# Graph attention layer on one core: turned adjacency blocks evacuated later in ScalarE's order, first loads in another order

## The chip, the cores and the metric

One NeuronCore of a Trainium2 chip. The metric is device time in microseconds (us). Before the change it is 1793.12 us, the median of three runs (1792.2 to 1793.35).

## What is computed

A graph attention layer over N = 8192 nodes with 128 features and H = 4 heads of 32, then a residual and a layer norm:

```
Wh      = x @ W.T                       (8192, 4, 32)
score_l = sum(Wh * a_l), score_r = sum(Wh * a_r)
e       = leaky_relu(score_l[n] + score_r[m], 0.2), where adj[n, m] + eye > 0, else -inf
out     = elu(softmax(e over m) @ Wh)
y       = layernorm(x + out)
```

adj is an 8192 x 8192 matrix of zeros and ones in float32, 256 MB. Because leaky_relu has two slopes, exp(e) is a product of a factor of n and a factor of m on either side of e = 0. The kernel therefore needs for each head only two 0/1 masks per pair of nodes: adjacent with e >= 0 (`bmask`), and adjacent with e < 0 (`cmask`). Each multiplies its own set of weighted values (`vt`, later read back from DRAM into `vring`) on TensorE.

## The kernel before, in words

**Units of work.** The output rows are cut into 4 chunks of 2048 (two halves of 1024). There are 16 passes of 32 steps, 512 steps in all. Passes 0 to 3 take one half of chunk 0 and two heads each ("narrow"); passes 4 to 15 take a whole chunk and one head ("wide"). A step q covers 256 of the columns m. Per step:

- *compare* (L479 ScalarE, L681 VectorE): makes the 0/1 mask of score_l against score_r into `bmask` from `lrow`, the row scores copied to all partitions. A step is four instructions in a narrow pass and two in a wide one; `on_vector` (L78) says how many of them VectorE does. ScalarE runs AH = 3 steps ahead in its own order (L524), and at most BR = 6 steps ahead of TensorE (L485, L486).
- *mask_b* and *mask_c* on VectorE (L703, L718): and with the adjacency bits, into `bmask` and `cmask`. `cmask` has CR = 3 buffers, so mask_c waits for the products of three steps before.
- *step* on TensorE (L391): 32 products with `bmask`, then the turns of adjacency blocks due in this step, then 32 products with `cmask`.

**Adjacency blocks.** The adjacency comes as 128 blocks of 1024 x 512 float32 (2 MB). SyncE loads a block in two parts into `abuf`, which has two buffers (`load_block`, L216; it waits until the block before the last one has been turned). TensorE turns it, transposed and packed four bits to a byte, into `trp`, a single PSUM bank (`turn_block`, L365). ScalarE copies `trp` into the cache `acache` (`evacuate`, L453). `turn_block(n)` waits for the evacuation of n - 1 (L368), because `trp` has no second buffer. `FIRST_TURNS` and `LATER_TURNS` (L54, L56) set the step in which a block is turned: blocks 2 to 15 in pass 0, blocks 16 to 63 with 2 or 3 steps between them (steps 32 to 144), blocks 64 to 127 with 3 or 4 (steps 148 to 393). ScalarE evacuates a block that was turned in step q at position q + 1 of its own order, behind compare(q + 4). After step 393 no block is left, and passes 13 to 15 have no turns.

**The end of a pass.** VectorE takes the sums from PSUM (L731, L735), which waits for TensorE's last products of the pass; then it weighs, adds and normalises in small pieces over the next steps. In passes 4, 8 and 12 the rows of a finished chunk are normalised in steps 13 to 20 (ScalarE, L502).

**The setup.** The values of x come in 16 groups (`load_x`, L212; a ring of six). TensorE transposes a group and projects it, VectorE takes the scores, ScalarE copies Wh. After every fourth group the row scores of a chunk are transposed, copied (`copy_l` of VectorE, L587) and stored to DRAM (`store_l`, L225). `load_lrow(0)` reads those of chunk 0 back. In SyncE's order it stands behind group 13, with a wait for the store (L286). Then VectorE makes the weighted values (`weigh`, L622; `rest`, L637; `lowest`, L644) together with ScalarE (`highest`, `middle`, L468, L475), for which ScalarE first makes `vv` (L511 to L513). SyncE's list of first loads is L278 to L292.

Each engine works strictly in the order written out by hand in its own block; nothing is reordered.

Of the kernel before, what the change touches and what calls it, by code (L numbers as in the profile page):

```python
# [6 lines left out]
def gat_kernel(nc, x, adj, W, a_l, a_r, out):  # L7
# [10 lines left out]
    NC = N // CHUNK  # L18
# [3 lines left out]
    QUADS = NT // BITS  # L22
# [41 lines left out]
    TURNED = [turned_at(q) for q in range(Q)]  # L64
    assert [n for t in TURNED for n in t] == list(range(AHEAD, NB))


    DIAGONALS = [(c, k // 2, 4 * c + k) for c in range(NC) for k in range(4)]

# [8 lines left out]
    def on_vector(q):  # L78

        w, s = WHERE[q]  # L80
        if s % 4 == 3:
            return 0
        if w == 0:
            return 0 if s < 2 else 2 if s % 2 == 0 and s % 8 != 6 else 1
        if w == 1:
            return 0 if s < 6 else (2 if s % 3 == 0 else 1)
        if narrow(w):
            return 0 if s < 5 else 1 if s % 5 == 0 else 2
        return 0 if s < 6 or s in (10, 17, 22, 29) or (w % 4 == 0 and s in (8, 9)) else 1
# [22 lines left out]
    with ctx:  # L112
# [98 lines left out]
        def _(sp):  # L211
# [13 lines left out]
            def store_l(c):  # L225
                sp.wait_ge(l_copied, c + 1)
                sp.dma_start(l_dram[c].rearrange("h j p -> (h j) p"), l_t[0:H * JC, c]).then_inc(l_stored, 16)

            def load_lrow(w):

                if w >= 2:
                    sp.wait_ge(cmp_act, (w - 1) * STEPS)
                    sp.wait_ge(cmp_dve, ON_VECTOR[(w - 1) * STEPS])
                c, half, h = UNITS[w][0]
                if narrow(w):
                    src = l_dram[c:c + 1, h:h + 2, half * SUB:(half + 1) * SUB].rearrange("o u j n -> o u (j n)").to_broadcast([P, 2, HALF])
                    sp.dma_start(lrow[:, w % 2], src).then_inc(lrow_in[w % 2], 16)
                else:
                    src = l_dram[c:c + 1, h].rearrange("o j n -> o (j n)").to_broadcast([P, CHUNK])
                    sp.dma_start(lrow[:, w % 2].rearrange("p u n -> p (u n)"), src).then_inc(lrow_in[w % 2], 16)  # L240
# [25 lines left out]
            def load_xr(c, half):  # L266
                for s in range(2):
                    sp.dma_start(zz[s::2, half * SUB:(half + 1) * SUB], as_bytes(x, c, half, s)).then_inc(xr_in, 16)
# [8 lines left out]
            sp.dma_start(acol[:, 1:2], a_r.rearrange("h (k o) -> (h k) o", o=1)).then_inc(a_in, 16)  # L277
            for g in range(XG):  # L278
                load_x(g)
                if g in (8, 11, 14, 15):  # L280
                    k = (8, 11, 14, 15).index(g)
                    load_block(k // 2, [k % 2])
                if g == 11:
                    store_l(0)
                if g == 13:
                    sp.wait_ge(l_stored, 16)  # L286
                    load_lrow(0)
            load_xr(0, 0)
            for c in range(1, NC):
                store_l(c)  # L290

            loaded, turned = 2, AHEAD  # L292
            for q in range(Q):
                w, s = WHERE[q]
                while loaded < NB and loaded - 1 <= turned:
                    load_block(loaded)
                    loaded += 1
                if w < JUST_MADE and s % EVERY_STEPS == 1:
                    store_v(q // EVERY_STEPS)
                if JUST_MADE * STEPS <= q + VR - 1 < Q:  # L300
                    load_v(q + VR - 1)
                turned += len(TURNED[q])
                if s == 3 and w + 1 < PASSES:
                    if w == 0:
                        sp.wait_ge(l_stored, 16 * NC)
                    load_lrow(w + 1)
                if w == 2 and s == 4:
                    sp.wait_ge(v_lo, JUST_MADE * NG)
                    load_xr(0, 1)
                if w == 2 and s == 22:  # L310
                    store_y(0, 0, ROWS_DONE[1])
                if w % 4 == 0 and w > 0:
                    c = w // 4
                    if s == 24:
                        for half in range(2):
                            if (c - 1, half) != (0, 0):
                                store_y(c - 1, half, ROWS_DONE[c + 1])
                    if s == 28:
                        sp.wait_ge(y_stored, 32 * 2 * c)
                        for half in range(2):  # L320
                            load_xr(c, half)
# [116 lines left out]
        def _(act):  # L438
# [68 lines left out]
            for g in range(XG):  # L507
                copy_wh(g)
                if g == 13:
                    compare(0)  # L510
            act.wait_ge(dr_done, 1)  # L511
            for b, scale in enumerate((1.0, SLOPE)):
                nc.scalar.activation(vv[:, :, :, b], dr[:, :, :], ACT.Exp, scale=scale).then_inc(vv_done, 1)  # L513
            evacuate(0)
            evacuate(1)
            highest(0)
            copy_l()
# [4 lines left out]
            for q in range(Q):  # L522
                w, s = WHERE[q]
                if q + AH < Q:  # L524
                    compare(q + AH)
                if q > 0:
                    for n in TURNED[q - 1]:
                        evacuate(n)
                if q == 2:
                    act.wait_ge(um_done, 1)  # L530
                    for b in range(2):
                        nc.scalar.activation(uu[:, :, b].rearrange("p c h j -> p c (h j)"), um[:, b], ACT.Exp).then_inc(uu_done, 1)
                if q % EVERY_STEPS == 1 and q // EVERY_STEPS + 1 < JUST_MADE * NG:
                    middle(q // EVERY_STEPS + 1)
                if q % EVERY_STEPS == 3 and q // EVERY_STEPS + 2 < JUST_MADE * NG:
                    highest(q // EVERY_STEPS + 2)
                if s == 5 and w > 0:
                    elu_exp(w - 1)
                for e, (done, js) in enumerate(FINISHED):
                    if w == done + 1 and 13 <= s < 13 + len(js) // 2:  # L540
                        normalise(e, js[2 * (s - 13):2 * (s - 13) + 2])
# [6 lines left out]
        def _(dve):  # L548
# [38 lines left out]
            def copy_l(c):  # L587
                dve.wait_ge(l_tr, c + 1)
                nc.vector.tensor_copy(l_t[0:H * JC, c].rearrange("p (w s) -> p s w", s=2),
                                      psum[0:H * JC, BANKS - 1, 0:P].rearrange("p (s w) -> p s w", s=2)).then_inc(l_copied, 1)  # L590
# [26 lines left out]
            dve.wait_ge(rmax_done, 1)  # L617
            r_top = rmax.rearrange("p (o h) -> p o h", o=1).to_broadcast([P, NT, H])
            nc.vector.tensor_tensor(dr[:, :, :], r_all, r_top, ALU.subtract).then_inc(dr_done, 1)
            copy_l(NC - 1)  # L620

            def weigh(n):  # L622
                h, g = 2 * (n // NG), n % NG
# [203 lines left out]
            def mean_part(e):  # L827
# [2 lines left out]
                nc.vector.scalar_tensor_tensor(nmr[:, js[0]:js[-1] + 1], mv[:, js[0]:js[-1] + 1, 0], -1.0, vrs[:, js[0]:js[-1] + 1],  # L830
                                               ALU.mult, ALU.mult).then_inc(nmr_done, 1)

            weigh(0)
            add_diagonal(0, 0)
            add_diagonal(0, 1)
            rest(0)
            compare(0)
            mask_b(0)
            lowest(0)
            compare(1)  # L840
# [134 lines left out]
```

## Time and profile before

| | |
|---|---|
| median of three runs | 1793.12 us (1792.2 to 1793.35) |
| the profiled execution | 1793.73 us, its span 1791.9 us |
| TensorE products / weight loads, busy | 1651.9 / 1628.6 us (92% / 91%) |
| VectorE, busy | 1685.0 us (94%) |
| ScalarE, busy | 1667.2 us (93%) |
| granted TensorE clock | 0.986 of full speed |

The busy times are sums over the span. The three compute engines are nearly equally full, so the table alone does not say which of them sets the end. In the rows below, PE is TensorE's products, PEld its weight loads, DVE VectorE, ACT ScalarE and SP or SPq SyncE's queue; L463 is line 463 of the kernel; "x4" is a number of instructions, and "a <- b" in a wait means that a waited for b. "issue" means that the profile shows nothing that the engine waited for.

### The profile page before, as it was taken

Reading aid. Unit: us, or ns where it says so; the run is one execution under the profiler, and the core shown is the slowest. Engines: PE = TensorE matmul, PEld = TensorE weight load, DVE = VectorE, ACT = ScalarE, POOL = GpSimd, SP = SyncE. Lnnn points to the kernel's source line nnn. Section 1 sums busy time; section 2 is a strip of 40 time slices with the busy share of each in tenths; the row PEclk is TensorE's granted clock in tenths of the full one; section 3 lists DMA queues with packets and bytes.
Section 4 is the critical chain, followed back from the end, with each engine's and each line's share of the span. In section 5 each row is a group of like instructions: output and inputs, shape, how many; then the busy total and the mean of one; then the engine's idle time right before and its main releaser. Section 6 shows DMA issues by size and latency. Waiting matters only on the chain. (4 is left out here: it accounts for less than half of the span.)

```text
span 1791.9 us, 80971 instructions
## 1 busy us (share of the span) xinstructions
PE 1651.9 (92%) x37067; PEld 1628.6 (91%) x37067; DVE 1685.0 (94%) x1903; ACT 1667.2 (93%) x1248; POOL 26.2 (1%) x36
## 2 busy tenths in 40 slices
PE   7698888999899999999999999999999999999995
PEld 6688788899899999999999999999999898999995
DVE  4999999998989989999998989999899999999997
ACT  3999999889899999999999999998999999999992
POOL 0000000000001000000000100000000100000000
PEclk9899999999999999999999999999999999999998
DMA  7996787999999786675766676666767131111111
GB/s 231 349 352 220 270 279 261 331 314 329 308 305 315 244 265 192 207 242 184 239 208 215 202 237 199 219 212 209 229 191 244 34 83 56 39 58 37 34 37 36
DMA packets 241476, 368.10 MB, mean 205 GB/s; under 512 B 12912, under 2 KB 103408, under 8 KB 239600
## 3 DMA queue, kind: packets, MB, share of 16 engines
q1 hardware_dynamic: 241136, 362.92, 62.3%
q8 instruction: 292, 4.78, 1.1%
q14 instruction: 48, 0.39, 0.1%
HBM read 345.57 MB, written 17.30 MB: 203 GB/s over the span
## 5 line engine op out<-in xcount | busy, mean ns | idle before, releaser
L494 ACT ACTIVATE bmask<-lrow,rtab 128x2048 fp8e4<-128x2048 f32 (+1 forms) x977 | 1544.4, 1662 | 9.4 <-PE psum L403 8.6
L403 PE MATMUL psum<-vring,cmask 128*128 128x99 bf16 x14336 | 718.6, 208 | 42.5 <-DVE cmask L721 33.2
L403 PE MATMUL psum<-vring,bmask 128*128 128x99 bf16 x14336 | 720.5, 208 | 10.1 <-DMA vring<-v_scratch 5.1
L403 PEld LDWEIGHTS psum<-vring,cmask 128*128 128x128 fp8e4 x14336 | 661.4, 98 | 55.7 <-DVE cmask L721 43.7
L403 PEld LDWEIGHTS psum<-vring,bmask 128*128 128x128 fp8e4 x14336 | 668.5, 97 | 12.4 <-issue 6.2
L716 DVE SCALAR_TENSOR_TENSOR bmask<-acache,bmask 128x1024 int32<-128x1024 int32 x512 | 624.2, 1219 | 50.1 <-ACT bmask L494 44.7
L721 DVE SCALAR_TENSOR_TENSOR cmask<-acache,bmask 128x1024 int32<-128x1024 int32 x512 | 623.2, 1217 | 3.0 <-PE psum L403 3.0
L697 DVE TENSOR_SCALAR bmask<-lrow,rtab 128x2048 fp8e4<-128x2048 f32 (+1 forms) x303 | 315.3, 1054 | 0.0
L372 PE MATMUL trp<-pack,abuf 128*128 128x64 bf16 x4096 | 143.1, 193 | 22.8 <-issue 12.9
L372 PEld LDWEIGHTS trp<-pack,abuf 128*128 128x128 bf16 x4096 | 131.7, 98 | 24.8 <-issue 22.7
L463 ACT CAST acache<-trp 128x512 int16<-128x512 f32 x128 | 73.9, 577 | 56.8 <-PE trp L372 56.5
L403 PE MATMUL psum<-vt,cmask 128*128 128x99 bf16 x2048 | 106.1, 210 | 21.9 <-DVE cmask L721 13.8
L403 PEld LDWEIGHTS psum<-vt,cmask 128*128 128x128 fp8e4 x2048 | 97.0, 99 | 24.7 <-DVE cmask L721 15.5
L403 PE MATMUL psum<-vt,bmask 128*128 128x99 bf16 x2048 | 106.3, 211 | 11.3 <-DVE vt L647 5.2
L403 PEld LDWEIGHTS psum<-vt,bmask 128*128 128x128 fp8e4 x2048 | 98.1, 99 | 12.5 <-issue 12.2
L727 DVE TENSOR_REDUCE acc<-psum 128x165 f32<-128x495 f32 (+1 forms) x112 | 61.7, 621 | 20.9 <-PE psum L403 20.9
L446 ACT COPY acache<-psum 128x256 f32<-128x256 f32 x32 | 10.4, 375 | 22.2 <-DVE acache L585 22.2
L946 POOL TENSOR_TENSOR vrs<-mv,epsc 128x8 f32<-128x8 f32 (+1 forms) x6 | 4.9, 813 | 1719.0 <-DVE mv L824 1719.0
L500 ACT ACTIVATE late<-late 128x512 f32<-128x512 f32 (+1 forms) x17 | 10.3, 603 | 21.1 <-DVE late L790 21.1
L505 ACT ACTIVATE late<-late,nmr,vrs 128x128 f32<-128x128 f32 x56 | 24.1, 483 | 4.7 <-DVE nmr L830 4.7
L642 DVE TENSOR_TENSOR late<-vring,vt 128x1056 f32<-128x1056 f32 x16 | 20.0, 1253 | 3.4 <-ACT vt L466 3.4
L634 DVE TENSOR_TENSOR vring<-acache,vv 128x528 f32<-128x528 f32 x32 | 21.1, 702 | 0.6 <-ACT vv L513 0.6
(64 smaller groups left out, 268.4 us busy)
## 6 DMA issues: line engine op xcount, KB each, us to landing
abuf<-in_adj_dram SPq DMA_DIRECT2D x256, 1024.0 KB, 8.3
vring<-v_scratch SPq DMA_DIRECT2D x384, 99.0 KB, 3.2
lrow<-l_scratch SPq DMA_DIRECT2D x16, 1024.0 KB, 7.7
v_scratch<-vt SPq DMA_DIRECT2D x16, 792.0 KB, 11.1
vring<-v_scratch SPq DMA_DIRECT2D x64, 198.0 KB, 6.7
cmask<-in_x_dram SPq DMA_DIRECT2D x16, 256.0 KB, 5.0
late<-in_x_dram SPq DMA_DIRECT2D x16, 256.0 KB, 5.3
out_dram<-late SPq DMA_DIRECT2D x16, 256.0 KB, 3.6
```

The costliest lines, as they stand in the source:

```text
L372: last = nc.tensor.matmul(trp[:, j * P // 2:(j + 1) * P // 2], block_hi, pack[:, k], start=(k == 0 and j == 0), stop=True, skip_group_chec ...
L403: return nc.tensor.matmul(psum[:, bank, at * S3:(at + 1) * S3], mask[:, j * P:(j + 1) * P], values, start=opening, stop=True, skip_group_c ...
L446: nc.scalar.copy(wh[:, at:at + 3:2].rearrange("p t (h e) -> p t h e", e=E)[:, :, :, 0:DK], both.rearrange("p t (h d) -> p t h d", d=DK)).t ...
L463: nc.scalar.copy(acache[:, c % 2, half, m].bitcast(i16), trp[:, :]).then_inc(evac_done, 1)
L494: last = nc.scalar.activation(to, rows, ACT.Relu, bias=rtab[:, 2 * s + i, H + h:H + h + 1], scale=BIG, saturate=False)
L505: nc.scalar.activation(zz[:, j], zz[:, j], ACT.Identity, bias=nmr[:, j:j + 1], scale=vrs[:, j:j + 1]).then_inc(y_ready, 1)
L634: last = nc.vector.tensor_tensor(v5[:, :, :, b], w4, vb, ALU.mult)
L642: nc.vector.tensor_tensor(vr, vf, dst[:, :, 0:E], ALU.subtract).then_inc(v_rest, 1)
L697: last = nc.vector.tensor_scalar(to, rows, rtab[:, 2 * s + i, h:h + 1], None, ALU.is_ge, saturate=False)
L716: nc.vector.scalar_tensor_tensor(m, adj_words(q), bit_of(q), m, ALU.bitwise_and, ALU.bitwise_and).then_inc(b_ready, 1)
L721: nc.vector.scalar_tensor_tensor(mask_words(cmask[:, q % CR]), adj_words(q), bit_of(q), mask_words(bmask[:, q % BR]), ALU.bitwise_and, ALU ...
L727: nc.vector.tensor_reduce(acc[:, START[b]:START[b] + n], psum[:, b, 0:n * S3].rearrange("p (i s e) -> p i e s", s=3, e=E), AX.X, ALU.add). ...
```

## The change

Four things are edited.

1. ScalarE's order: a block turned in step q is evacuated at position q + 1 (blocks 2 to 15, as before), q + 2 (blocks 16 to 63) or q + 3 (blocks 64 to 127).
2. SyncE's first loads: the two parts of block 0 stand behind groups 8 and 10, the first part of block 1 behind group 13. The wait for the store of the row scores, `load_lrow(0)` and the second part of block 1 stand behind all groups of x. The stores of the other row scores and the loads of blocks 2 and 3 are interleaved. The load of the residual's rows (`load_xr(0, 0)`) goes to step 10.
3. Compare of step 0: two of its four instructions go from ScalarE to VectorE. VectorE does them ahead of `weigh(0)`, and `copy_l` of the last chunk behind it.
4. ScalarE evacuates block 0 ahead of making `vv`.

```diff
--- before.py
+++ after.py
@@ -64,6 +64,13 @@
     TURNED = [turned_at(q) for q in range(Q)]
     assert [n for t in TURNED for n in t] == list(range(AHEAD, NB))
 
+    def emptied_after(n):
+
+        return 1 if n < QUADS else 2 if n < 4 * QUADS else 3
+
+    EMPTIED = [[n for d in (1, 2, 3) if q >= d for n in TURNED[q - d] if emptied_after(n) == d] for q in range(Q)]
+    assert [n for e in EMPTIED for n in e] == list(range(AHEAD, NB))
+
 
     DIAGONALS = [(c, k // 2, 4 * c + k) for c in range(NC) for k in range(4)]
 
@@ -81,7 +88,7 @@
         if s % 4 == 3:
             return 0
         if w == 0:
-            return 0 if s < 2 else 2 if s % 2 == 0 and s % 8 != 6 else 1
+            return 2 if s == 0 else 0 if s < 2 else 2 if s % 2 == 0 and s % 8 != 6 else 1
         if w == 1:
             return 0 if s < 6 else (2 if s % 3 == 0 else 1)
         if narrow(w):
@@ -277,19 +284,21 @@
             sp.dma_start(acol[:, 1:2], a_r.rearrange("h (k o) -> (h k) o", o=1)).then_inc(a_in, 16)
             for g in range(XG):
                 load_x(g)
-                if g in (8, 11, 14, 15):
-                    k = (8, 11, 14, 15).index(g)
+                if g in (8, 10, 13):
+                    k = (8, 10, 13).index(g)
                     load_block(k // 2, [k % 2])
                 if g == 11:
                     store_l(0)
-                if g == 13:
-                    sp.wait_ge(l_stored, 16)
-                    load_lrow(0)
-            load_xr(0, 0)
-            for c in range(1, NC):
-                store_l(c)
-
-            loaded, turned = 2, AHEAD
+            sp.wait_ge(l_stored, 16)
+            load_lrow(0)
+            load_block(1, [1])
+            store_l(1)
+            store_l(2)
+            load_block(2)
+            store_l(3)
+            load_block(3)
+
+            loaded, turned = 4, AHEAD
             for q in range(Q):
                 w, s = WHERE[q]
                 while loaded < NB and loaded - 1 <= turned:
@@ -304,6 +313,8 @@
                     if w == 0:
                         sp.wait_ge(l_stored, 16 * NC)
                     load_lrow(w + 1)
+                if w == 0 and s == 10:
+                    load_xr(0, 0)
                 if w == 2 and s == 4:
                     sp.wait_ge(v_lo, JUST_MADE * NG)
                     load_xr(0, 1)
@@ -508,10 +519,10 @@
                 copy_wh(g)
                 if g == 13:
                     compare(0)
+            evacuate(0)
             act.wait_ge(dr_done, 1)
             for b, scale in enumerate((1.0, SLOPE)):
                 nc.scalar.activation(vv[:, :, :, b], dr[:, :, :], ACT.Exp, scale=scale).then_inc(vv_done, 1)
-            evacuate(0)
             evacuate(1)
             highest(0)
             copy_l()
@@ -523,9 +534,8 @@
                 w, s = WHERE[q]
                 if q + AH < Q:
                     compare(q + AH)
-                if q > 0:
-                    for n in TURNED[q - 1]:
-                        evacuate(n)
+                for n in EMPTIED[q]:
+                    evacuate(n)
                 if q == 2:
                     act.wait_ge(um_done, 1)
                     for b in range(2):
@@ -617,7 +627,6 @@
             dve.wait_ge(rmax_done, 1)
             r_top = rmax.rearrange("p (o h) -> p o h", o=1).to_broadcast([P, NT, H])
             nc.vector.tensor_tensor(dr[:, :, :], r_all, r_top, ALU.subtract).then_inc(dr_done, 1)
-            copy_l(NC - 1)
 
             def weigh(n):
                 h, g = 2 * (n // NG), n % NG
@@ -830,11 +839,12 @@
                 nc.vector.scalar_tensor_tensor(nmr[:, js[0]:js[-1] + 1], mv[:, js[0]:js[-1] + 1, 0], -1.0, vrs[:, js[0]:js[-1] + 1],
                                                ALU.mult, ALU.mult).then_inc(nmr_done, 1)
 
+            compare(0)
             weigh(0)
+            copy_l(NC - 1)
             add_diagonal(0, 0)
             add_diagonal(0, 1)
             rest(0)
-            compare(0)
             mask_b(0)
             lowest(0)
             compare(1)
```

## Rows read from the trace of the kernel before

**Rows 1.** Passes 1, 2, 5, 8, 12, 13: stretch, us; busy PE, PEld, DVE, ACT, POOL (instructions); clock, DMA share, GB/s.

```profile
174.50:298.50 124.00, 106.73 (x2428) 104.15 (x2426) 121.81 (x138) 124.00 (x128) 0.00 (x0) 0.99 0.77 260
298.50:416.90 118.40, 108.06 (x2482) 106.44 (x2480) 106.49 (x136) 107.40 (x116) 3.16 (x2) 0.99 0.95 313
...
639.90:741.80 101.90, 100.01 (x2309) 99.28 (x2306) 98.40 (x95) 97.56 (x59) 0.00 (x0) 1.00 0.69 220
...
944.90:1052.40 107.50, 99.83 (x2266) 98.67 (x2263) 101.34 (x132) 106.91 (x76) 5.69 (x2) 0.98 0.68 216
...
1363.80:1471.00 107.20, 99.19 (x2215) 97.34 (x2213) 101.45 (x130) 107.20 (x74) 5.69 (x2) 1.00 0.34 102
1471.00:1569.00 98.00, 93.59 (x2052) 92.01 (x2050) 98.00 (x96) 96.51 (x52) 0.00 (x0) 1.00 0.17 47
```

**Rows 2.** Waits over the whole span: who waited for whom, us, times, longest.

```profile
ACT acache L463 <- PE trp L372: 56.5, 47, 3.7
...
DVE bmask L716 <- ACT bmask L494: 44.7, 38, 2.4
...
PE trp L372 <- ACT acache L463: 8.2, 2, 5.9
```

**Rows 3.** Waits of passes 2 and 3 (290 to 534 us).

```profile
PE psum L403 <- issue: 9.3, 13, 1.4
PE trp L372 <- issue: 8.9, 9, 1.5
```

**Rows 4.** SyncE's DMA issues in the setup: start us, us, engine line op.

```profile
18.45 1.13 SPq L214 DMA_DIRECT2D cmask<-in_x_dram  x2
23.99 0.37 SPq L237 DMA_DIRECT2D lrow<-l_scratch  x1
...
25.47 0.87 SPq L214 DMA_DIRECT2D cmask<-in_x_dram  x1
...
27.72 3.74 SPq L268 DMA_DIRECT2D late<-in_x_dram  x2
```

**Rows 5.** DMA issues of the first 60 us: count, size, median us to landing.

```profile
cmask<-in_x_dram SPq DMA_DIRECT2D x16, 256.0 KB, 5.0
lrow<-l_scratch SPq DMA_DIRECT2D x1, 1024.0 KB, 6.1
```

**Rows 6.** TensorE in the setup, in order of time; idle before a row in brackets.

```profile
30.85 0.66 PE L343 MATMUL psum<-identf,cmask 128*128 128x128 f32 x4 [3.17 <-DMA cmask<-in_x_dram]
...
35.39 1.12 PE L343 MATMUL psum<-identf,cmask 128*128 128x128 f32 x4 [2.63 <-DMA cmask<-in_x_dram]
```

**Rows 7.** ScalarE in the setup, in order of time.

```profile
33.64 4.27 ACT L494 ACTIVATE bmask<-lrow,rtab 128x1024 fp8e4<-128x1024 f32 x4
...
39.90 0.65 ACT L446 COPY acache<-psum 128x256 f32<-128x256 f32 x2 [0.58 <-DVE acache L585]
```

**Rows 8.** VectorE at the end of the setup, in order of time.

```profile
42.31 1.33 DVE L634 TENSOR_TENSOR vring<-acache,vv 128x528 f32<-128x528 f32 x2 [0.61 <-ACT vv L513]
...
45.63 1.26 DVE L642 TENSOR_TENSOR late<-vring,vt 128x1056 f32<-128x1056 f32 x1 [0.71 <-ACT vt L466]
...
53.43 1.41 DVE L697 TENSOR_SCALAR bmask<-lrow,rtab 128x1024 fp8e4<-128x1024 f32 x2
```

**Rows 9.** Waits in pass 12 (1364 to 1462 us).

```profile
DVE bmask L716 <- ACT bmask L494: 5.3, 6, 1.3
```

**Rows 10.** Waits in pass 8 (956 to 1047 us).

```profile
DVE bmask L716 <- issue: 1.7, 3, 1.3
DVE bmask L716 <- ACT bmask L494: 1.4, 2, 1.0
```

**Rows 11.** ScalarE in pass 1 around the evacuation of block 17.

```profile
197.20 0.58 ACT L463 CAST acache<-trp 128x512 int16<-128x512 f32 x1
...
198.66 7.40 ACT L494 ACTIVATE bmask<-lrow,rtab 128x1024 fp8e4<-128x1024 f32 x7
```

**Rows 12.** TensorE in pass 1: the turn of block 18.

```profile
200.07 1.09 PE L372 MATMUL trp<-pack,abuf 128*128 128x64 bf16 x32
```

## The prediction

> **What bounds the kernel now.** Begin with the busy times by pass [rows 1]. The passes without turns (13 to 15) take 98.0 us, and VectorE is busy for all of it: 98.0 us is VectorE's own work in a wide pass. A wide pass with turns is longer, and it is not the same engine that makes it so. In pass 5 (101.9 us) TensorE is busy 100.0 us, VectorE 98.4, ScalarE 97.6: TensorE sets the pace. In pass 12 ScalarE is busy 107.2 of 107.2 us and VectorE only 101.5; pass 8 is alike (106.9 of 107.5). There ScalarE sets the pace, because it also normalises a finished chunk. Pass 1 has ScalarE at 124.0 of 124.0 and VectorE at 121.8. In pass 2 TensorE is the fullest with 108.1 of 118.4.
>
> Next the waits [rows 2]. ScalarE stands 56.5 us waiting for a turn that it is to evacuate, and VectorE 44.7 us waiting for ScalarE's masks. The tempting reading is that the first causes the second, so that about 45 us can be had. The waits of passes 2 and 3 [rows 3] warn against it: TensorE loses 9.3 + 8.9 = 18.2 us there for nothing that a semaphore explains, often in the middle of a block's 32 matmuls, while the DMA engines are busy 0.95 of the time [rows 1]. In pass 2, TensorE's 108.1 us of work and its half of these 18.2 make 117.2 of 118.4 us. ScalarE waits there because TensorE is late, and an earlier mask doesn't make TensorE faster.
>
> Last the setup. SyncE has issued x groups 12 and 13 by 19.6 us, then stands until 23.99 for the store of the row scores [rows 4]. Groups 14 and 15 are issued behind that, and TensorE waits 3.17 and 2.63 us for them [rows 6].
>
> **The change part by part: the setup.** Without the wait in front of them, groups 14 and 15 are issued at about 20 and 21 us (behind half a block of 1 MB, and a slot in the ring of six must be free). A group lands in 5.0 us [rows 5], even 7 us would do: TensorE wants group 14 at 30.85 - 3.17 = 27.7 us [rows 6]. Both waits go, 5.8 us.
>
> The row scores' read then stands behind the groups. It still waits for the store, so it is issued at 23.99 us as now, and lands 6.1 us later [rows 4, 5], at about 30.1. ScalarE's compare(0) starts there and not at 33.64, and has two instructions in place of four: 2.1 us in place of 4.27 [rows 7]. Then the copies of two Wh groups (0.65 us each [rows 7]), and the evacuation of block 0 and the two small instructions of vv, which I put at as much again: done by about 34.8 us. VectorE's two instructions of compare(0) cost 1.4 us (the pair in [rows 8]) and lie in its wait for vv. So `weigh(0)` begins near 34.8 instead of 42.31 [rows 8], 7.5 us earlier. The evacuation of block 1 is then done before `weigh(0)` ends, so the 0.7 us that VectorE still waits ahead of `rest(0)` at 45.63 [rows 8] mostly goes too. I take **8.0 us** for the setup. Lower bound: if the read lands as late after its issue as group 15 did (issued at 25.47 [rows 4], turned at 35.39 [rows 6]: 9.9 us), the chain is 3.8 us later: 4.2. Upper bound 10, if the store lands sooner as well.
>
> Is it kept? From there ScalarE and VectorE are both nearly full to the end of pass 1 [rows 1], so the whole sequence moves with its start. Blocks 2 and 3 are issued earlier too. The store of the last row scores waits for `copy_l` behind `weigh(0)`, and block 3 is queued behind it in SyncE's order, near 38 us; its turn is due some 15 us later, which covers it. The residual's load, 3.74 us of SyncE's time [rows 4], goes into step 10, where only block loads stand behind it. They have about 7 us of room. If that cover is gone, TensorE's lag grows by about 1.5 us.
>
> **The later evacuations, pass by pass.** ScalarE's 56.5 us of waits nearly all go: at position q + 3 it has just done compare(q + 6), which needed the first half of step q anyway, and the turn follows that half at once. Between 47 waits that is 1.2 us each [rows 2]. What ScalarE can win by it is bounded, since six buffers of `bmask` let it run six steps ahead of TensorE and no more. Following its order through the ends of passes 7 and 11 with that limit, it reaches passes 8 and 12 about 2.6 and 3.5 us earlier relative to TensorE.
>
> - Pass 12: VectorE waits 5.3 us for masks; 1.3 of them (the longest) lie before the sums of pass 11 are taken, where it would wait for TensorE instead. Of the other 4.0 [rows 9] I take **3.5**, ScalarE's new lead. After step 393 nothing but VectorE's own work is left, so this stays won.
> - Pass 8: 1.4 + 1.7 = 3.1 us [rows 10], of which the lead pays **2.6**. The rest of the pass has TensorE waiting for DMA reads, untouched.
> - Passes 5 to 7 and 9 to 11: TensorE is busy 100.0 of 101.9 us [rows 1]. VectorE's waits for masks turn into waits for TensorE's last products. I take 0; below that nothing, above it 2 us in all.
> - Pass 13 on: VectorE is full. 0.
>
> **What the later evacuation can cost.** `trp` is one bank, so the next turn waits for an evacuation that now stands behind one more compare (two more for blocks 64 up). Of the turns of blocks 16 to 63, 29 follow another after only two steps, 21 of them in passes 2 to 4. Block 17 shows the price: it is evacuated at 197.20, and compare(39), its first four of seven instructions, runs from 198.66 [rows 11] for 4.3 us. In its new place the evacuation ends at 203.5, while the turn of block 18 began at 200.07 [rows 12]: 3.4 us of TensorE's time, with its 32 products behind it. In pass 1 TensorE has 17 us of slack against 124, so I book nothing. In passes 2 to 4 ScalarE is further ahead; three or four of the 21 would still be caught by about a microsecond, less its new lead. I take **1.5 us** lost. Both ends: 0, and 6.
>
> Before, TensorE waited for an evacuation in two places, 8.2 us [rows 2]. The Trainium skill, page "PSUM — Partial Sum Buffer", section "Summary: rules for kernel authors", says to evacuate promptly. It speaks against this change; these rows agree that waiting can cost, and the slower rival below is what it would come to.
>
> **Sum:** -8.0 - 3.5 - 2.6 + 1.5 = -12.6 us, from the profiled 1793.73 to 1781.1. The median of before lies 0.6 us below its profiled run; so does my number: **1780.5 us**.
>
> **The rivals.**
> - *Only the setup pays.* TensorE and the DMA-loaded passes absorb everything else: 1793.1 - 8 = 1785.1 us. For it: 100.0 of 101.9. Against: pass 12 has ScalarE full and VectorE with 5.7 us idle.
> - *Every wait for masks comes back.* 1793.1 - 8.0 - 44.7 = 1740.4 us. It needs TensorE to keep up, and 100.0 of 101.9 us says it can't. The Trainium skill, page "Perfetto Trace Analysis", section "Identifying the Most-Contended Engine", would have me optimise the engine of the highest occupancy first. That is VectorE by this table, and the rule read over the whole span leads to this rival; by pass, the rows disagree with it.
> - *The setup's gain is eaten.* The read of the row scores is late behind x and half a block, the bound of 4.2 holds, and the close turns cost 6 where passes 8 and 12 give 4: about 1790.9 us, hardly to be told from no change.
> - *Slower: the single PSUM bank.* Were each of the 21 close turns in passes 2 to 4 held up by 1.3 us (block 18 would be by 3.4), TensorE, which sets the pace there, loses 27 us: 1793.1 - 8.0 - 6.1 + 27 = 1806 us. It decides from (8.0 + 6.1) / 21 = 0.7 us for each turn. Against it: in these passes ScalarE has been waiting for the turn, 11 us in pass 2 alone (118.4 - 107.4), so it is ahead, not behind.
> - That the change doesn't do what it says I see no way to: all blocks keep their turns and due steps.
>
> **How the numbers follow.** Forecast 0.60, only the setup 0.18, all waits back 0.06, setup eaten 0.10, slower 0.06. A measurement of this kernel can tell about 0.2% (3.6 us) from no change. Faster by more: 0.60 + 0.18 + 0.06 = 0.84; within: 0.10; slower: 0.06. The range takes in the forecast with its bounds (setup 4.2 to 10, passes 8 and 12 with 2 to 8.4, cost 0 to 6) short of their extremes together, and the second case: 1773 to 1788 us, leaving out the two extreme rivals and part of the fourth.
>
> **What would show it.** Right: TensorE's waits for x gone, `weigh(0)` near 35 us, and `rest(0)` near 37.5; ScalarE's wait for turns under 10 us in place of 56.5; VectorE's wait for its masks down, but its wait for TensorE's last products (`acc`) up; passes 5 to 7 within 1 us of today's length; passes 8 and 12 shorter by about 3. Wrong: passes 5 to 7 shorter by 2 us or more each (then TensorE wasn't their bound), or TensorE's wait for evacuations above 10 us in passes 2 to 4, or compare(0) starting after 33 us.

## The result and the profile after

The changed kernel takes 1786.75 us (median of 9 runs, 1785.55 to 1789.62) against 1793.29 (9 runs of the kernel before): ratio 0.9952, interval 0.9932 to 0.9972. The ratio is over all these runs; the two medians alone are 6.5 us apart. Two later comparisons, on two different chips, gave 0.9932 (0.9914 to 0.9950) and 0.9943 (0.9925 to 0.9961). The three have the mean 0.9942, which is 10.3 us. The forecast was 12.6 us, with a range of 5 to 20.

The page of the changed kernel, its span and busy times:

```profile
span 1784.3 us, 80971 instructions
...
PE 1649.9 (92%) x37067; PEld 1626.8 (91%) x37067; DVE 1685.1 (94%) x1905; ACT 1667.3 (93%) x1246; POOL 26.2 (1%) x36
```

The same work is done in 7.6 us less. The windows by pass, for the stretches that answer to [rows 1] (passes 1, 2, 5, 8, 12, 13; busy PE, PEld, DVE, ACT, POOL; clock, DMA share, GB/s):

```profile
168.70:292.70 124.00, 105.18 (x2335) 102.71 (x2333) 121.73 (x138) 124.00 (x128) 0.00 (x0) 0.96 0.78 260
292.70:408.80 116.10, 103.31 (x2398) 101.58 (x2394) 106.49 (x135) 107.97 (x116) 3.15 (x2) 1.00 0.95 315
634.30:737.20 102.90, 100.31 (x2311) 99.45 (x2309) 98.38 (x97) 97.22 (x59) 0.00 (x0) 1.00 0.69 218
941.90:1048.10 106.20, 100.56 (x2299) 99.39 (x2296) 101.22 (x131) 105.03 (x76) 5.68 (x2) 0.99 0.69 218
1357.60:1463.50 105.90, 100.13 (x2243) 98.53 (x2240) 101.12 (x132) 104.65 (x73) 5.69 (x2) 1.00 0.36 107
1463.50:1561.50 98.00, 93.60 (x2052) 92.01 (x2049) 98.00 (x97) 96.53 (x52) 0.00 (x0) 1.00 0.18 47
```

These stretches go from VectorE's first mask of a pass to that of the next. Passes 8 and 12 are 1.3 us shorter each (106.2 for 107.5, 105.9 for 107.2), ScalarE is no longer busy for all of pass 12 (104.65 of 105.90), pass 5 is 1.0 us longer, and passes 1 and 13 are as long as before. Now the waits over the whole span, which answer to [rows 2]:

```profile
DVE acc L736 <- PE psum L414: 41.4, 15, 4.3
...
ACT bmask L505 <- PE psum L414: 37.4, 61, 1.4
PE psum L414 <- DVE cmask L730: 36.0, 55, 2.3
...
DVE cmask L730 <- PE psum L414: 25.0, 26, 2.4
ACT acache L474 <- PE trp L383: 21.8, 15, 2.8
...
PE trp L383 <- ACT acache L474: 11.7, 7, 5.5
...
DVE bmask L725 <- ACT bmask L505: 3.0, 3, 1.6
```

And four of the kernel before that aren't in [rows 2]:

```profile
PE psum L403 <- DVE cmask L721: 47.0, 66, 2.3
...
DVE acc L727 <- PE psum L403: 20.9, 15, 3.2
...
ACT bmask L494 <- PE psum L403: 8.6, 12, 0.9
...
DVE cmask L721 <- PE psum L403: 3.0, 5, 1.5
```

VectorE's wait for masks has fallen by 41.7 us (44.7 to 3.0). Its wait for TensorE's last products has risen by 20.5 (20.9 to 41.4), and its wait for a free `cmask` by 22.0 (3.0 to 25.0). Together that is 42.5: taken over the whole kernel, the wait only got another name. TensorE's own wait for `cmask`, which is what a late mask costs the products, fell by 11.0 (47.0 to 36.0). ScalarE's wait for turns fell by 34.7 (56.5 to 21.8), its wait for TensorE to release a `bmask` rose by 28.8 (8.6 to 37.4): the limit of six steps.

The setup. SyncE's issues, the landing of the row scores' read (count, size, us), TensorE's remaining waits for x, then ScalarE and VectorE in order of time (start, us, and in brackets the idle time before):

```profile
19.86 3.08 SPq L221 DMA_DIRECT2D cmask<-in_x_dram  x2
23.26 0.53 SPq L244 DMA_DIRECT2D lrow<-l_scratch  x1
23.84 0.48 SPq L229 DMA_DIRECT2D abuf<-in_adj_dram  x1
```

```profile
lrow<-l_scratch SPq DMA_DIRECT2D x1, 1024.0 KB, 8.6
```

```profile
23.06 0.66 PE L354 MATMUL psum<-identf,cmask 128*128 128x128 f32 x4 [0.69 <-DMA cmask<-in_x_dram]
...
28.48 0.66 PE L354 MATMUL psum<-identf,cmask 128*128 128x128 f32 x4 [0.98 <-DMA cmask<-in_x_dram]
```

```profile
31.91 2.19 ACT L505 ACTIVATE bmask<-lrow,rtab 128x1024 fp8e4<-128x1024 f32 x2 [0.85 <-DMA lrow<-l_scratch]
34.01 1.17 ACT L457 COPY acache<-psum 128x256 f32<-128x256 f32 x4
35.05 0.62 ACT L474 CAST acache<-trp 128x512 int16<-128x512 f32 x1
35.52 0.79 ACT L525 ACTIVATE vv<-acache 128x256 f32<-128x256 f32 x2
```

```profile
34.37 1.41 DVE L706 TENSOR_SCALAR bmask<-lrow,rtab 128x1024 fp8e4<-128x1024 f32 x2
36.34 1.33 DVE L643 TENSOR_TENSOR vring<-acache,vv 128x528 f32<-128x528 f32 x2 [0.57 <-ACT vv L525]
...
38.91 1.26 DVE L651 TENSOR_TENSOR late<-vring,vt 128x1056 f32<-128x1056 f32 x1 [0.64 <-ACT vt L477]
```

The waits for x are 0.69 and 0.98 us in place of 3.17 and 2.63 [rows 6]. The read is issued at 23.26 and lands 8.6 us later, not 6.1 [rows 5]. `weigh(0)` starts at 36.34 (42.31 before) and `rest(0)` at 38.91 (45.63 before), 6.7 us earlier [rows 8].

### The profile page after: what moved, and what is told of

It is laid out like the page before. It is cut to its first block and busy times, and to the rows that moved or that the text cites. A ratio compares the mean times of both kernels' runs of the same rounds, so it can differ in the third digit from the quotient of the medians.

```text
span 1784.3 us, 80971 instructions
## 1 busy us (share of the span) xinstructions
PE 1649.9 (92%) x37067; PEld 1626.8 (91%) x37067; DVE 1685.1 (94%) x1905; ACT 1667.3 (93%) x1246; POOL 26.2 (1%) x36
## 5 line engine op out<-in xcount | busy, mean ns | idle before, releaser
L505 ACT ACTIVATE bmask<-lrow,rtab 128x2048 fp8e4<-128x2048 f32 (+1 forms) x975 | 1548.0, 1667 | 39.4 <-PE psum L414 37.4
L730 DVE SCALAR_TENSOR_TENSOR cmask<-acache,bmask 128x1024 int32<-128x1024 int32 x512 | 633.1, 1237 | 25.1 <-PE psum L414 25.0
L725 DVE SCALAR_TENSOR_TENSOR bmask<-acache,bmask 128x1024 int32<-128x1024 int32 x512 | 633.8, 1238 | 6.7 <-ACT bmask L505 3.0
L706 DVE TENSOR_SCALAR bmask<-lrow,rtab 128x2048 fp8e4<-128x2048 f32 (+1 forms) x305 | 321.8, 1071 | 0.0
L414 PE MATMUL psum<-vt,cmask 128*128 128x99 bf16 x2048 | 106.5, 210 | 15.1 <-DVE cmask L730 7.5
L414 PE MATMUL psum<-vt,bmask 128*128 128x99 bf16 x2048 | 106.2, 211 | 13.4 <-DVE acc L736 4.9
L736 DVE TENSOR_REDUCE acc<-psum 128x165 f32<-128x495 f32 (+1 forms) x112 | 61.8, 628 | 41.4 <-PE psum L414 41.4
L474 ACT CAST acache<-trp 128x512 int16<-128x512 f32 x128 | 73.8, 577 | 21.8 <-PE trp L383 21.8
L516 ACT ACTIVATE late<-late,nmr,vrs 128x128 f32<-128x128 f32 x56 | 24.2, 487 | 7.2 <-DVE nmr L839 7.2
L511 ACT ACTIVATE late<-late 128x512 f32<-128x512 f32 (+1 forms) x17 | 10.3, 607 | 21.1 <-DVE late L799 21.1
L457 ACT COPY acache<-psum 128x256 f32<-128x256 f32 x32 | 10.2, 375 | 18.1 <-DVE acache L595 18.1
```

The costliest lines, as they stand in the source:

```text
L414: return nc.tensor.matmul(psum[:, bank, at * S3:(at + 1) * S3], mask[:, j * P:(j + 1) * P], values, start=opening, stop=True, skip_group_c ...
L474: nc.scalar.copy(acache[:, c % 2, half, m].bitcast(i16), trp[:, :]).then_inc(evac_done, 1)
L505: last = nc.scalar.activation(to, rows, ACT.Relu, bias=rtab[:, 2 * s + i, H + h:H + h + 1], scale=BIG, saturate=False)
L511: nc.scalar.activation(em[:, rows], em[:, rows], ACT.Exp).then_inc(em_done, 1)
L516: nc.scalar.activation(zz[:, j], zz[:, j], ACT.Identity, bias=nmr[:, j:j + 1], scale=vrs[:, j:j + 1]).then_inc(y_ready, 1)
L706: last = nc.vector.tensor_scalar(to, rows, rtab[:, 2 * s + i, h:h + 1], None, ALU.is_ge, saturate=False)
```

## The experiments

There were twelve further runs: seven other versions, three of them measured twice, and the changed kernel itself twice more. Ratios are to runs of the kernel before on the same chip. "Gain" is worked out from the ratio.

### The setup alone

The changed kernel, with every block evacuated one step after its turn.

```diff
-        return 1 if n < QUADS else 2 if n < 4 * QUADS else 3
+        return 1
```

> The changed kernel with every block evacuated at position q + 1 again, as before. My theory (TensorE sets the pace in the passes with turns, passes 8 and 12 are ScalarE's): the setup alone gives -6.7 us at rest(0), some 5 to 6 of it kept, so 1787 to 1788 us; VectorE's waits for masks are back at 40 to 45 us; passes 8 and 12 are as long as before (107.5 and 107.2 us). Rival (the late evacuations lose in passes 4 to 7 what they win in 8 and 12): the same or faster than the changed kernel, 1785 to 1787 us. Rival (they carry the gain): above 1790 us.

Measured: 1789.99 us against 1793.66, ratio 0.9980 (0.9969 to 0.9991): 3.6 us, less than `rest(0)` had gained and 2 us above the 1787 to 1788 expected, at the edge of the rival in which the late evacuations carry the gain. The rest came as expected: VectorE waits 43.5 us for masks again, and the stretches of passes 8 and 12 are 107.5 and 107.2 us, as before.

### The later evacuations alone

The kernel before, with the list `EMPTIED` (built as in the change, cut here) for ScalarE and nothing else of the change.

```diff
...
-                if q > 0:
-                    for n in TURNED[q - 1]:
-                        evacuate(n)
+                for n in EMPTIED[q]:
+                    evacuate(n)
```

> The kernel before with only the late evacuations (positions q + 2 and q + 3), its old first loads and its old compare(0). My theory: passes 8 and 12 shorter by 1.4 each, passes 4 to 7 longer or equal: the net is 0 to -3 us, 1790 to 1793 us. ScalarE's waits for turns fall from 56.5 to near 22 us and VectorE's waits for masks from 44.7 to near 3 us although the time hardly moves. Rival (the waits for masks bind): -6 us or more, below 1787 us.

Measured: 1789.61 us against 1793.66, ratio 0.9974 (0.9960 to 0.9989): 4.7 us, more than the 0 to 3 expected and less than the rival's 6. The waits went as expected: ScalarE waits 21.6 us for turns, VectorE 3.8 for masks.

### Blocks 16 to 63 early again

```diff
-        return 1 if n < QUADS else 2 if n < 4 * QUADS else 3
+        return 1 if n < 4 * QUADS else 3
```

> The changed kernel with blocks 16 to 63 evacuated at q + 1 again, and only blocks 64 to 127 at q + 3. Theory that the close turns of blocks 16 to 63 cost TensorE time (its waits for evacuations rose from 8.2 to 11.7 us): pass 4 is shorter by about 2 us than in the changed kernel and the whole 1 to 3 us faster than it. Rival (pass 4 is longer by chance of the DMA and issue stalls, not by the evacuations): no difference, 1786 to 1787 us.

Measured: 1783.42 us, ratio 0.9943 (0.9931 to 0.9956). TensorE has no wait for an evacuation in pass 1 here (3.6 us in the changed kernel). Against the first median of the changed kernel it looks 3 us better, but the two were not measured side by side, and pass 4, which was expected to be 2 us shorter, is not (110.6 us for 110.8 on TensorE).

### Half of each later turn

The turns of blocks 64 and up with 16 of their 32 products, which leaves out half of the adjacency bits of those blocks.

```diff
-                for k in range(BITS):
+                for k in range(0, BITS, 2 if n >= 4 * QUADS else 1):
```

> The changed kernel, in which a turn of blocks 64 to 127 makes only 16 of its 32 matmuls (bits 0 and 2), so half of their adjacency bits are left out. TensorE has 0.46 us less work for each of these turns, 8.2 of which fall in a pass. If TensorE sets the pace in passes 5 to 7 and 9 to 11, each of them is 3 to 3.7 us shorter (102 to 103 goes to 99 to 100), and the whole about 20 to 25 us less. If VectorE or ScalarE sets it, they stay within 1 us.

One run: 1770.96 us. Pass 5, from TensorE's first product to that of pass 6, in the changed kernel and in this one:

```profile
645.30:748.00 102.70, 100.11 (x2306) 99.32 (x2305) 97.78 (x95) 97.02 (x59) 0.00 (x0) 1.00 0.67 214
```

```profile
647.20:745.90 98.70, 96.47 (x2181) 95.59 (x2179) 97.62 (x95) 95.45 (x57) 0.00 (x0) 1.00 0.69 223
```

TensorE loses 3.6 us of work, the pass loses 4.0, and VectorE (97.62 of 98.70) is the next bound. Passes 5 to 7 are together 9.5 us shorter (296.9 for 306.4), passes 9 to 11 are 8.1 shorter (299.2 for 307.3). TensorE sets their pace: it is idle for only 2.6 of pass 5's 102.7 us, and no more than that could be had by freeing VectorE or ScalarE. The whole kernel fell by less than the 20 to 25 us expected, 15.2 by the spans of the two traces (1784.3 and 1769.1), since VectorE takes over as the bound and passes 9 to 11 gave 2.7 us each and not 3 to 3.7.

### The changed kernel once more

> The changed kernel once more, unedited, on the chip of the other runs of this call, so that it can be set against the kernels that follow. If blocks 16 to 63 are what holds it back, it is 1786 to 1788 us here and 2 to 4 us above its sister with only blocks 64 up evacuated later (1783.4 us before). If that kernel was only lucky in its chip, both come out within 1 us of each other. TensorE's waits for evacuations in pass 1 are again 3.5 to 4.5 us.

Measured: 1782.11 us against 1794.98, ratio 0.9932 (0.9914 to 0.9950). The same program is 4.6 us below its first median, so the 3 us of the version above say nothing yet. TensorE's waits for evacuations in pass 1 are there again, 5.4 us.

### The residual's load later

To the version with blocks 16 to 63 early:

```diff
-                if w == 0 and s == 10:
+                if w == 0 and s == 26:
                     load_xr(0, 0)
```

> Late evacuation for blocks 64 up only, and the residual's load at step 26 of pass 0, where no block is left to load, in place of step 10. Theory that 0.5 MB amid the block loads costs TensorE time in pass 0 (the start of pass 1 kept 5.8 of the 6.7 us won in the setup): pass 0 is 0.5 to 1.5 us shorter and the whole 1782 to 1783 us. Rival (the load lies beside the rest, and pass 0 lost it elsewhere): no difference from 1783.4 us.

Measured: 1783.33 us, ratio 0.9942 (0.9924 to 0.9961), with pass 0 as long as in its parent (127.7 us from VectorE's first mask to that of pass 1, in both). The load in step 10 costs nothing.

### The first half of block 1 behind the read

To the same version:

```diff
-                if g in (8, 10, 13):
-                    k = (8, 10, 13).index(g)
+                if g in (8, 10):
+                    k = (8, 10).index(g)
...
-            load_block(1, [1])
+            load_block(1)
```

> Late evacuation for blocks 64 up only, and the first half of block 1 behind the read of the row scores in place of behind group 13. Theory (the setup fell 1.3 us short of my 8.0 because that read landed 8.6 us after its issue in place of 6.1, beside 1 MB of block 1): the read lands within 6.5 us, compare(0) starts at 30 to 30.5 us in place of 31.9, rest(0) at 37.5 in place of 38.9, and the whole is 1 to 1.5 us faster, 1782 us. Rival (block 1 is then late for its turn at 35.8 us and delays the second evacuation): no gain or a loss of 1 us.

Measured: 1783.99 us, ratio 0.9948 (0.9931 to 0.9966): no gain. Its read's landing, ScalarE in the setup, and TensorE's wait for block 1:

```profile
lrow<-l_scratch SPq DMA_DIRECT2D x1, 1024.0 KB, 6.3
```

```profile
30.41 2.20 ACT L505 ACTIVATE bmask<-lrow,rtab 128x1024 fp8e4<-128x1024 f32 x2
...
34.02 0.80 ACT L525 ACTIVATE vv<-acache 128x256 f32<-128x256 f32 x2
37.21 0.59 ACT L474 CAST acache<-trp 128x512 int16<-128x512 f32 x1 [2.40 <-PE trp L383]
```

```profile
PE trp L383 <- DMA abuf<-in_adj_dram: 3.1, 1, 3.1
```

The read lands in 6.3 us again, so it was the half block just ahead of it that made it 7.6 to 9.6 us in the other versions with the new setup. compare(0) starts 1.5 us earlier (30.41 for 31.91), `vv` too. But the turn of block 1 now waits 3.1 us for its data, ScalarE waits 2.40 for that turn, and `rest(0)` starts at 38.83, where it was (38.91). The DMA engines are at least 0.9 busy in every slice of 1.5 us from 12 to 46 us of this trace, and what one load gained another lost.

### Fewer bytes in passes 1 to 4

To the changed kernel. The second part of blocks 16 to 63 is loaded for one tile of rows in four, so 3/8 of those blocks' bytes are left out and TensorE turns old data in their place.

```diff
+                    few = part == 1 and QUADS <= n < 4 * QUADS
+                    tiles = 1 if few else SUB // 2
...
-                                 rows.rearrange("(j p) m -> p j m", p=P)).then_inc(a_loaded[n % 2], 16)
+                                 rows.rearrange("(j p) m -> p j m", p=P)[:, 0:tiles]).then_inc(a_loaded[n % 2], 16)
```

> The changed kernel, in which the second half of blocks 16 to 63 is loaded for one row tile of four, so 3/8 of their bytes and of their adjacency are left out. If TensorE's unexplained stalls (issue; 27 us in passes 0 to 4 after the setup, 17.6 in passes 2 and 3) come from DMA engines that are nearly full, they fall to under 5 us in passes 2 and 3 together, which end some 12 us earlier. If they are TensorE's own, they stay at 15 to 18 us.

One run: 1769.4 us. Passes 2 and 3 from TensorE's first product on, and TensorE's waits in them: first the changed kernel, then this one.

```profile
305.40:534.50 229.10, 211.23 (x4928) 208.32 (x4929) 208.33 (x248) 211.01 (x217) 3.15 (x2) 1.00 0.96 318
```

```profile
PE trp L383 <- issue: 9.0, 9, 1.5
PE psum L414 <- issue: 8.5, 12, 1.2
...
PE trp L383 <- ACT acache L474: 0.3, 1, 0.3
```

```profile
302.00:521.20 219.20, 210.62 (x4932) 209.31 (x4929) 209.16 (x251) 211.52 (x218) 3.16 (x2) 0.99 0.78 238
```

```profile
PE psum L416 <- issue: 3.5, 4, 1.4
PE trp L385 <- ACT acache L476: 3.2, 2, 2.7
PE trp L385 <- issue: 1.7, 2, 1.3
```

With the DMA engines 0.78 busy in place of 0.96, TensorE's stops without any releaser fall from 17.5 to 5.2 us, and the two passes from 229.1 to 219.2, though the number of TensorE's instructions is the same. That is close to what was expected (under 5 us, and 12 us earlier), and against stops of TensorE's own. In passes 5 to 7 (DMA engines 0.67 busy in the changed kernel) such stops come to less than 1 us together in every trace.

The traces also tell what ends a stop. In the changed kernel's passes 2 and 3 the DMA engines carry 38 packets that the profile calls instruction, of 16,384 bytes each:

```profile
q8 instruction: 38, 0.62, 1.1%
```

One comes every 6 us, yet each of the 21 stops ends 1.3 to 1.6 us after the end of such a packet. In the same passes of all 14 traces (the kernel before, the changed one and the twelve further runs) it is 262 stops of 262, at 1.2 to 1.7 us. The packets are TensorE's: leaving out half of each later turn took away 1,024 products and as many weight loads, and with them 8 of the 241 packets of passes 0 to 12, one for every 256 instructions. So the stops are instructions that come late, behind full DMA engines. The packets themselves take 1.0 us here and 1.1 with fewer bytes; what holds up their start is not shown. The Trainium skill, page "Runtime: NRT & Kernel Launch", section "Instruction fetch mechanics", says that an engine's sequencer fetches its instructions by DMA in blocks of 16 KiB, and calls the cost of this mostly hidden. The packets agree with the blocks; in passes 2 and 3 the cost is not hidden.

### All four versions on one chip

Setup alone, evacuations alone, both, and both with blocks 16 to 63 early: the kernels of above, beside the kernel before (1794.24 us), all on one chip.

> The setup's edits alone, on one chip with the three versions that follow, so that chips don't differ between them. The earlier ratios were 0.9980 for the setup alone, 0.9974 for the later evacuations alone, and 0.9952 and 0.9932 for both. Theory 1 (the parts add, each keeps what its own run showed): 0.998, both together 0.995. Theory 2 (the setup's 6.7 us earlier start is kept nearly whole, and the earlier run fell low): 0.9963 or lower here. Theory 3 (the setup's start is kept only where the later evacuations are there too, since without them ScalarE holds VectorE up again in passes 2 to 4): here 0.998 or more, and both together below 0.9945, by more than the two parts come to.

> The later evacuations alone, same chip. Theory 1: 0.9974 again (4.7 us). My forecast's terms (2.6 + 3.5 - 1.5 = 4.6 us) also give 0.9974. Theory 3: above 0.998 when taken with a both-together version below 0.9945.

> The changed kernel, third measurement. Theory 1: 0.995 (9 us less 0 to 1). Theory 3: 0.993, 4 us or more below the sum of the two parts. If it comes to 0.995 here and the two parts to 0.998 and 0.9975, they add, and 0.9932 was a run on a favourable chip.

> Changed kernel with blocks 16 to 63 evacuated one step after the turn's step, blocks 64 to 127 three. Theory A (evacuating 16 to 63 late costs TensorE 3 to 6 us in passes 1 and 2 and that is kept): 3 us or more below the changed kernel on this chip. Theory B (those waits lie in TensorE's slack): within 1.5 us of it.

| version | median us | ratio | interval | gain by the ratio, us |
|---|---|---|---|---|
| setup alone | 1788.85 | 0.9962 | 0.9943 to 0.9980 | 6.8 |
| evacuations alone | 1791.03 | 0.9991 | 0.9973 to 1.0009 | 1.6 |
| both | 1784.51 | 0.9943 | 0.9925 to 0.9961 | 10.2 |
| both, 16 to 63 early | 1785.19 | 0.9946 | 0.9928 to 0.9964 | 9.7 |

The setup alone gives the 0.9963 of theory 2, but its interval reaches up to theory 3's 0.998, and both together lie just below theory 3's 0.9945: these ratios alone don't decide between them; the stretches of the traces below do. The evacuations alone came out lower than in their first run, 1.6 for 4.7 us, with intervals that overlap, and here alone they can't be told from no change. The parts come to 8.4 us and both together to 10.2, within the error of either. Blocks 16 to 63 early or late: 0.5 us apart, theory B. The 3 us between their first medians were the comparison, not the version.

The waits of the two single versions, setup alone first:

```profile
ACT acache L474 <- PE trp L383: 60.6, 47, 3.4
...
DVE bmask L725 <- ACT bmask L505: 43.6, 36, 2.6
...
DVE acc L736 <- PE psum L414: 22.1, 15, 3.2
```

```profile
DVE acc L734 <- PE psum L411: 41.8, 15, 4.6
...
ACT acache L471 <- PE trp L380: 22.4, 16, 3.1
...
PE trp L380 <- ACT acache L471: 12.7, 8, 5.6
```

With the setup alone the waits of before are all there [rows 2]; with the evacuations alone they are those of the changed kernel. So the exchange of waits is the evacuations' doing, and the earlier start is the setup's.

### The traces read together

Medians differ by a few us between comparisons of the same two kernels. Stretches of a trace tell more. TensorE's order is the same in all, so each of the twelve traces with the whole computation (ten of the further runs, the changed kernel, the one before) can be cut at its first product of a pass (us; "first" is the first product of all):

| kernel | first | pass 0 | passes 1 to 7 | passes 8 to 12 |
|---|---|---|---|---|
| before | 49.6 | 133.7 | 770.6 | 522.7 |
| setup alone, first run / one chip | 43.6 / 42.8 | 135.0 / 134.6 | 772.6 / 774.3 | 521.8 / 523.0 |
| evacuations alone, first run / one chip | 48.7 / 51.3 | 133.7 / 134.4 | 774.6 / 774.5 | 517.3 / 514.5 |
| changed kernel, first / once more / one chip | 42.9 / 43.8 / 43.5 | 134.7 / 135.2 / 134.7 | 774.1 / 771.4 / 775.0 | 517.4 / 515.8 / 514.3 |
| 16 to 63 early, first run / one chip | 44.1 / 43.3 | 133.8 / 134.2 | 771.6 / 775.2 | 516.9 / 517.2 |
| the same, residual later / block 1 behind | 43.7 / 42.8 | 133.8 / 133.2 | 772.9 / 773.3 | 515.9 / 515.9 |

Passes 13 to 15 take 294.3 us in every one.

- **Start of pass 1** (first and pass 0 together): 183.8 us on average in the three with the old setup, 177.7 in the nine with the new one. The setup's edits bring 6.1 us. At the start of pass 8 the three are at 953.9 to 960.2 us and the nine at 949.3 to 953.2: 5.9 us apart on average, so the start is kept, with the later evacuations and without.
- **Passes 8 to 12**: 522.5 in the three with evacuations one step after, 516.1 in the nine where blocks from 64 on are late, and no value of one group reaches into the other. The evacuations bring 6.4 us there. Pass 12 alone is 104.6 to 104.7 against 102.2 in all nine. TensorE's wait for `cmask` in these five passes is 14.8 to 16.7 us in the three and 10.9 to 12.9 in the nine.
- **Passes 1 to 7**: from 770.6 to 775.2, in no order that an edit explains. The changed kernel alone has 771.4, 774.1 and 775.0. The five with blocks 16 to 63 late average 773.9, the seven others 772.9.

The trace of before happens to have the shortest passes 1 to 7 of all twelve. That is why the changed kernel's first trace is only 7.5 us ahead at the start of pass 13: 6.7 at the first product, 1.0 lost in pass 0, 3.5 lost in passes 1 to 7, 5.3 won in passes 8 to 12 (rounded, they add up to 7.5).

## Why the prediction was right, and where it was off

Point by point, by its own steps:

- **The setup, 8.0 us.** Right in its mechanism: the waits for x go (0.69 and 0.98 us are left), compare(0) starts before 33, `weigh(0)` and `rest(0)` at 36.34 and 38.91 for "near 35" and "near 37.5". Off in one term, "lands 6.1 us later". That figure was measured with no half block just ahead of the read. With half of block 1 there, the read took 7.6 to 9.6 us, and the chain starts at 31.9 and not 30.1. I had the lower bound for just this (9.9 us, 4.2 gained) and took the other end. So `rest(0)` gained 6.7 us and not 8.0, and 6.1 were kept at pass 1.
- **Pass 12, 3.5 us, and pass 8, 2.6.** Pass 12 gave 2.5 on TensorE (104.7 to 102.2). In its window VectorE's wait for masks went from 5.3 [rows 9] to 1.0, and its wait for the sums of pass 11 from 0.9 to 3.4, which I had allowed for with 1.3:

```profile
DVE acc L736 <- PE psum L414: 3.4, 1, 3.4
...
DVE bmask L725 <- ACT bmask L505: 1.0, 1, 1.0
```

  On TensorE pass 8 took 109.5 to 111.6 us in the three traces with evacuations one step after, and 106.5 to 108.4 in the nine others, so 2.8 less on average. A part of that is clock: the mean granted clock of pass 8 was 0.97 or 0.98 in all of the three and 0.98 in three of the nine, and at 0.98 on both sides the pass took 109.5 and 109.9 against 107.9 to 108.3. Passes 9 to 11, where I had booked 0, gave another 1.0 on average, in ranges that overlap (306.9 to 308.0 and 305.0 to 307.4). Passes 8 to 12 together gave 6.4, where I had 6.1: the places are right, but that the sum comes out so close is partly luck, with pass 12 lower and passes 9 to 11 higher. The two leads of ScalarE, 2.6 and 3.5 us, were worked out, and no run measured them.
- **Passes 5 to 7 and 9 to 11, 0.** Right for passes 5 to 7. The windows show pass 5 at 102.9 for 101.9, and halving the turns showed whose bound it is. The size of the waits that changed their name (42.5 us) is what this step predicted: they would turn into waits for TensorE's last products. The half of it that became a wait for a free `cmask` (22.0) I had not named, though that too is a wait for products. It comes from blocks 16 to 63: with these early again it is 7.5 us, VectorE waits 24.2 for masks, and the time is the same.
- **Pass 1, nothing booked.** Right: 3.6 to 5.4 us of TensorE waiting for an evacuation, as worked out for block 18, and the pass is 124.0 us long as before.
- **Close turns in passes 2 to 4, 1.5 us lost.** The waits there are 0.3 to 1.4 us in the traces of the changed kernel. Whether passes 1 to 7 lose anything, 1.0 by the averages, can't be told from their spread of 4.6. The slower rival, which needed 0.7 us for each of 21 turns, is out. The Trainium skill, page "PSUM — Partial Sum Buffer", section "Summary: rules for kernel authors", says to evacuate promptly. In these traces not doing so cost TensorE waits of 3.6 to 5.4 us in pass 1 and 0.3 to 1.4 in passes 2 to 4, and no pass that is longer by more than the spread.
- **ScalarE's wait for turns under 10 us.** Wrong: 21.8. In passes 5 to 11, where the blocks are evacuated at q + 3 now, none of the 30.5 us is left. All 15 waits that remain are for blocks up to 63, and 12 of them, 18.2 us, for blocks 33 to 63 in passes 2 to 4, which are evacuated at q + 2: one position later was not enough. I had worked it out for q + 3 and taken it for all.
- **The rivals.** Every wait for masks back (1740.4): out, since they turned into waits for TensorE. Only the setup pays (1785.1): out by passes 8 to 12 in nine traces, though the first median alone, 1786.75, would have spoken for it. The setup's gain eaten: half right in its cause, the late read, and wrong in its size.

The sum by the traces is -6.1 - 6.4 + 1.0 = -11.5 us; the three comparisons of runs average -10.3, and the forecast was -12.6. Of the difference, 1.9 us are the setup's term; the rest is less than the runs can tell.

## What to carry to other kernels

A wait between two engines is worth only what the third one allows: look stretch by stretch at who is full, and count a removed wait only where the others have room. When a read is moved to stand beside a large load, don't take its old landing time, take the longest of its neighbours'. And when the gain is under 1%, compare stretches of several traces of both kernels: one trace of each mixes the change with nearly 5 us of drift, here in passes 1 to 7, that no edit explains.

## What the runs showed of the hardware

- TensorE stops in the middle of a run of products, with no semaphore behind it, while the DMA engines are 0.95 busy and more: 17.5 us in passes 2 and 3. With 3/8 of the adjacency's bytes left out there and the DMA engines 0.78 busy, 5.2. Each of these stops, 262 in 14 traces, ends 1.2 to 1.7 us after the end of a 16,384-byte packet of TensorE's instructions; the packets are 6 us apart.
- The 1 MB read of the row scores lands 6.0 to 6.9 us after its issue with no half block just ahead of it in the queue (4 traces), and 7.6 to 9.6 with one (10 traces).
- The same program on the same input has passes 1 to 7 between 771.4 and 775.0 us long. Passes 13 to 15, where the DMA engines are 0.17 to 0.18 busy and VectorE sets the pace, are 294.3 us in all twelve.
